# A macaron layer with two mixture-of-experts FFNs on one core: half the bias added on VectorE, TensorE's filling products redistributed, the logits of tiles 2 and 3 scored later, the first weight splits held behind the first gather

## The reference, cut to what matters

```
x = x + 0.5 * ffn(layernorm(x))        # first FFN,  f = 0
x = x + attention(layernorm(x))
x = x + 0.5 * ffn(layernorm(x))        # second FFN, f = 1

ffn(x):   logits = x @ router.T; the best 2 of 8 experts for each token, gates = softmax of the two
          out = sum over the 2 experts of gate * (silu(x @ wi_a.T) * (x @ wi_b.T)) @ wo.T
          return out + bias
attention: 16 heads of 16, causal, over 256 tokens, 4 batches; ctx @ w_o.T + b_o
```

## Time and profile before

| what | value |
|---|---|
| median of 3 runs | 430.71 us (430.55 to 431.05) |
| the profiled execution | 430.32 us |
| its span in the profile | 428.6 us |
| mean granted clock of TensorE | 0.975 |
| TensorE busy | 402.1 us, 94% |
| VectorE busy | 299.3 us, 70% |
| ScalarE busy | 257.1 us, 60% |
| GpSimd busy | 249.2 us, 58% |
| chain that ended last, by engine | TensorE 64%, VectorE 15%, DMA 8%, issue 5% |

### The profile page before, as it was taken

One profiled execution on the slowest core, in us unless ns is written; L12 is line 12 of the kernel. 1 busy time (PEld: TensorE's weight loads), 2 busy tenths in 40 slices (PEclk: granted clock), 3 DMA queues, 4 the chain that ended last, 5 costly groups with the idle time before them and its releaser, 6 DMA issues.

```text
span 428.6 us, 10138 instructions
## 1 busy us (share of the span) xinstructions
PE 402.1 (94%) x2892; PEld 331.2 (77%) x2893; DVE 299.3 (70%) x612; ACT 257.1 (60%) x640; POOL 249.2 (58%) x312
## 2 busy tenths in 40 slices
PE   7779999999999989799999999888899999999996
PEld 3558888888888767588888888674588888888884
DVE  6878997756655895877677676967356775566566
ACT  2737866565556455788788787722365555655552
POOL 5355457765478169577777677200555596654860
PEclk9889999999999999999999999966999999999999
DMA  7959911211111800000000000007641212112136
GB/s 253 400 143 397 363 55 40 66 44 61 55 46 38 271 32 2 1 3 3 2 0 0 0 0 0 2 1 254 208 153 50 61 40 66 57 49 55 43 99 219
DMA packets 22059, 38.90 MB, mean 91 GB/s; under 512 B 3217, under 2 KB 14737, under 8 KB 21777
## 3 DMA queue, kind: packets, MB, share of 16 engines
q1 hardware_dynamic: 17168, 24.41, 16.6%
q0 software_dynamic: 4576, 12.07, 9.4%
q10 hardware_dynamic: 288, 2.10, 1.3%
HBM read 29.37 MB, written 9.19 MB: 90 GB/s over the span
## 4 chain that ended last, share of the span: by engine, by line
PE 64%; DVE 15%; DMA 8%; issue 5%; ACT 3%; POOL 3%; ACTq 0%; SPq 0%; DVEq 0%; POOLq 0%
PE bank L1379 25%; PE bank L1401 12%; PE bank L1549 6%; PE bank L1389 4%; PE bank L1560 4%; DMA w_out<-y_scratch 3%; PE bank L1516 3%; PE bank L1355 2%; DMA unused_rows<-in_wr_t,own_row 2%; DMA arena<-xn_scratch,gather_row 1%; DVE arena L902 1%; DMA y_scratch<-arena,scatter_row 1%; DVE pT_lo L1185 1%; DVE v L1255 1%; PE bank L1550 1%
## 5 line engine op out<-in xcount | busy, mean ns | idle before, releaser
L533 POOL DMA_INDIRECT arena<-xn_scratch,gather_row x46 | 51.4, 1117 | 60.8 <-PE bank L1355 39.5
L539 POOL DMA_INDIRECT y_scratch<-arena,scatter_row x42 | 61.1, 1454 | 34.8 <-ACT arena L707 32.0
L1043 DVE TENSOR_TENSOR wo_lo<-w_out,wo_hi 128x1024 fp32r<-128x1024 f32 x46 | 61.2, 1330 | 4.1 <-PE bank L1401 2.5
L1379 PE MATMUL bank<-w_hi,xT_hi 128*128 x184 | 62.4, 421 | 0.0
L1048 DVE TENSOR_TENSOR gT_lo<-bank,gT_hi 128x512 fp32r<-128x512 f32 x46 | 31.7, 689 | 38.7 <-ACT gT_hi L681 38.7
L1379 PE MATMUL bank<-w_hi,xT_lo 128*128 x184 | 57.7, 394 | 0.0
L1379 PE MATMUL bank<-w_lo,xT_hi 128*128 x184 | 57.3, 392 | 0.0
L674 ACT ACTIVATE arena<-bank 128x512 f32<-128x512 f32 x46 | 27.5, 598 | 46.7 <-PE bank L1379 46.7
L619 POOL TENSOR_TENSOR k_head<-k_hi,head_mask 128x256 fp32r<-128x256 f32 x64 | 38.7, 625 | 28.1 <-PE bank L1550 21.0
L696 ACT ACTIVATE wo_hi<-w_out 128x1024 fp32r x46 | 48.8, 1061 | 5.5 <-issue 3.4
L1032 DVE TENSOR_TENSOR xT_lo<-bank,xT_hi 128x256 fp32r<-128x256 f32 x46 | 19.5, 424 | 35.8 <-ACT xT_hi L666 35.6
(11 more groups left out here) (197 smaller groups left out, 961.5 us busy)
## 6 DMA issues: line engine op xcount, KB each, us to landing
w_raw<-in_win_t SPq DMA_DIRECT2D x8, 1024.0 KB, 9.7
w_out<-in_wout_t SPq DMA_DIRECT2D x16, 512.0 KB, 7.8
w_out<-y_scratch SPq DMA_DIRECT2D x8, 512.0 KB, 6.2
xn_scratch<-arena ACTq DMA_DIRECT2D x2, 1024.0 KB, 6.0
x<-in_x SPq DMA_DIRECT2D x4, 256.0 KB, 3.7
out<-x SPq DMA_DIRECT2D x4, 256.0 KB, 2.1
arena<-xn_scratch,gather_row POOLq DMA_INDIRECT x46, 3.5
y_scratch<-arena,scatter_row POOLq DMA_INDIRECT x46, 3.0
```

The source lines that it names most:

```text
L533: pool.indirect_dma_start(out=xb[j % 2][:, :], out_offset=None, in_=xn_dram, in_offset=bass.IndirectOffsetOnAxis(ap=gather_row[:, j:j + 1] ...
L539: pool.indirect_dma_start(out=y_dram, in_=y[j % 2][:, :], in_offset=None, out_offset=bass.IndirectOffsetOnAxis(ap=scatter_row[:, j:j + 1], ...
L1043: dve.tensor_tensor(wo_lo[:, :, :], w_out[:, bass.ds(e, 1), :, :].rearrange("p o c d -> p (o c) d"), wo_hi[u][:, :, :].bitcast(F32), ALU.s ...
L1379: last = pe.matmul(bank[2 * half + u][:, :], tok[u][:, k, :], wts[:, bass.ds(e, 1), k, half * H:(half + 1) * H], start=(part == 0 and k == ...
```

## The change

It has five parts.

1. `bias_half` and GpSimd's `add_bias` of it go. VectorE adds half the bias itself, a pair of tiles at a time (`add_half_bias`): one pair after block 5's work, three pairs after block 6's.
2. The rehearsal goes, and with it GpSimd's wait for it.
3. VectorE holds its first splits (`split_low(0)`, `split_low(1)`) until GpSimd has raised `first_begun`, just behind its first gather.
4. The logits of tiles 2 and 3 in the second FFN are scored after the output projection and the transposes of tiles 4 and 5; `best_of` and `choose` of the first group move behind with them, `choose` behind the last `scale`.
5. The filling products change: one more after tiles 2 and 3 and one after tiles 4 and 5 of the first layer norm, 4 after the first FFN's last logits, 10 instead of 6 and 8 instead of 6 behind `plan_ready`; in the finish 3 between the two context transposes, 2 after the logits of tiles 4 and 5 in place of 2 before them, 1 before the last logits, and 4 instead of 2 after them.

```diff
-WARM_START, WARM_RANKS, WARM_PLAN, WARM_TURNED = 12, ((6, 5), (6, 5)), (6, 6), (4, 4)
-WARM_END, WARM_TURN2, WARM_CHOSEN = 2, 2, 2
+WARM_START, WARM_RANKS, WARM_PLAN, WARM_TURNED = 12, ((6, 5), (6, 5)), (10, 8), (4, 4)
+WARM_END = 2
 WARM_TURN = (5, 3)
-WARM_LN = (5, 1, 0, 0)
+WARM_LN = (5, 2, 1, 0)
+WARM_LAST = (4, 4)
+WARM_FINISH = (3, 2, 1)
...
-        bias_half = sb("bias_half", [P, D])
+        bias_row = sb("bias_row", [P, D])
...
@@ GpSimd
-            def rehearse():
-
-                then(pool.iota(own_row[:, :], [[0, 1]], base=0, channel_multiplier=1))
-                pool.indirect_dma_start(out=unused_rows[:, :], out_offset=None, in_=wr_in,
-                                        in_offset=bass.IndirectOffsetOnAxis(ap=own_row[:, 0:1], axis=0)).then_inc(rehearsed, 16)
...
-            rehearse()
...
             def ffn(f):
-                if f == 0:
-                    pool.wait_ge(rehearsed, 16)
                 pool.wait_ge(plan_ready, f + 1)
...
                 for j in range(AHEAD):
                     gather(f, j)
+                    if f == 0 and j == 0:
+                        pool.sem_inc(first_begun)
...
-                    if j == 6:
-                        if f == 0:
-                            pool.wait_ge(bias_loaded, 32)
-                            then(pool.tensor_scalar(bias_half[:, :], bias_half[:, :], 0.5, None, ALU.mult))
-                        add_bias(2 * f, bias_half)
-                    elif j == SCATTERED // 2:
+                    if j == SCATTERED // 2:
...
@@ VectorE
+            def add_half_bias(f, i):
+
+                dve.wait_ge(bias_loaded, 32)
+                dve.wait_ge(xn_ready, TILES * 2 * f + 2 * i + 2)
+                two = x[:, 2 * i:2 * i + 2, :]
+                dve.scalar_tensor_tensor(two, bc(bias_row[:, :], 1, [P, 2, D]), 0.5, two, ALU.mult, ALU.add)\
+                    .then_inc(bias_added, 1)
+
...
                 if f == 0:
+                    dve.wait_ge(first_begun, 1)
                     split_low(0)
                     split_low(1)
...
                     if isinstance(j, int) and j == PEELED - 2:
                         weigh_slots(f)
+                        add_half_bias(f, 0)
+                    if isinstance(j, int) and j == PEELED - 1:
+                        for i in range(1, TPAIRS):
+                            add_half_bias(f, i)
...
                 scale(2, 2)
-                best_at = best_of(1, 0)
...
                 sum_up(TPAIRS - 1, 1)
+                best_at = best_of(1, 0)
+                scale(2, TPAIRS - 1)
                 choose(0, best_at)
-                scale(2, TPAIRS - 1)
...
@@ TensorE, ffn(f): the part with f == 0, then the part with f == 1
                     score_experts(0, (TPAIRS - 1,))
+                    warm(WARM_LAST[0])
...
                         last.then_inc(xnT_in_psum, 1)
+                    warm(WARM_FINISH[2])
...
                     last.then_inc(logits_done, 1)
-                    warm(WARM_CHOSEN)
+                    warm(WARM_LAST[1])
...
@@ TensorE, finish()
                 turn_half(0)
-                score_experts(1, (1,))
+                warm(WARM_FINISH[0])
                 turn_half(1)
                 project_half(0)
                 project_half(1)
                 turn(2, (2,))
-                warm(WARM_TURN2)
+                score_experts(1, (1,))
 
                 pe.wait_ge(attn_added, BATCH + 1)
                 score_experts(1, (2,))
+                warm(WARM_FINISH[1])
```

More of the change, by code:

```diff
@@ L197, in build @@
         row_nos = sb("row_nos", [P, P], F16)
-        own_row = sb("own_row", [P, 1], I32)
-        unused_rows = sb("unused_rows", [P, E])
         blk_nos = sb("blk_nos", [P, BLOCKS + 1], F16)
@@ L283, in build @@
         half_hot = sem("half_hot")
-        rehearsed = sem("rehearsed")
+        first_begun = sem("first_begun")
         pairs_done = sem("pairs_done")
@@ L428, in _ @@
             load_w_out(E - 1)
-            for dst, src in ((bias_half, bias_in), (bo, bo_in)):
+            for dst, src in ((bias_row, bias_in), (bo, bo_in)):
                 sp.dma_start(dst[:, :], src.partition_broadcast(P)).then_inc(bias_loaded, 16)
```

## The result

The changed kernel takes **427.68 us** (median of 17 runs, 425.42 to 431.14) beside 430.62 of before (17 runs, 428.21 to 433.92): ratio 0.9947, 95% interval 0.9926 to 0.9969. Two further sets gave 427.45 and 427.47 us. It is faster, by 0.53% or 2.3 us by the ratio; the two medians differ by 2.9 us. 5.5 us were forecast.

What follows compares the result with a forecast made beforehand. TensorE's chain was taken to bound the whole program. The terms -1.1 (stall), -1.1 (start), +0.2, -2.9 (finish) and -0.6 (last logits) sum to -5.5 from 430.3: 424.8, median 425.2 us, range 424.0 to 428.9.

Steps and rivals of the forecast that it cites:

- sign: Whole kernel: faster, chance 0.9; same 0.05, slower 0.05.
- the start: First gather to block 0: rehearsal gone and splits held, gather lands 1.0 us sooner; -1.1 us, ends 0.2 and 1.6.
- handed over: Hold at the first gather: first_begun rises as the gather is handed over (21.5), xT_lo on time; gain 1.6 us.
- instruction ends: Hold at the first gather: first_begun rises when its instruction ends (22.4), hi*lo products wait 0.5; gain 1.1 us.
- Rival C: First gather: pays what the rehearsal paid, landing 7.52 us after its start instead of 3.31; median 429.8, chance 0.05.
- 0.5 earlier start: First gather: without the rehearsal GpSimd starts it at about 21.46 instead of 21.95 us.
- the last logits: Last logits of the finish: 1.73 to 0.96 us at full clock, less 0.15; -0.6 us, ends +0.5 and -0.8.
- The bias: Block 8, first FFN: GpSimd's bias add gone, so the stall goes, -1.1 us; bias on VectorE +0.2.
- the +0.2: Block 7, first FFN: three bias adds on VectorE make gT_lo end at 71.5, where TensorE wanted it at 71.29.
- The finish: First context transpose to the projection's closing addition: 6.16 us falls to about 3.2 at full clock; -2.9, ends -0.3 and -3.0.
- Rival A: Finish: clock stays low as now, finish gives -0.3 and tail -0.4; 427.6, median 428.0 us; chance 0.25.
- the logits' move alone: Finish: moving the logits of tiles 2 and 3 gives about 0.75 to 1.2 us of the -2.95, the rest the clock.

Runs made afterwards that it cites:

- the hold behind the instruction: Changed kernel with first_begun raised by a GpSimd memset behind the first gather: 428.86 us (0.9977); with xT_lo also behind expert 0's splits alone, 427.78 us (0.9976).
- finish alone: Before with only part 4 and the fillers of the finish and behind it, 8 instead of 6 behind the second plan_ready: 428.25 us (0.9968).
- moved logits without fillers: Changed kernel without the finish's new fillers, 2 instead of 4 behind the last logits, logits of tiles 2 and 3 still moved: 429.70 us (0.9964).
- bias alone: Before with only part 1, half the bias on VectorE and GpSimd's halving and add gone, run twice: 429.50 us (1.0001) and 427.96 us (0.9970).

## Why the prediction was right in sign and wrong in size

**The failed step: the start** (-1.1 predicted, about +0.7 measured). "So it ends near 22.4 instead of 23.44" took for granted that the hold keeps the splits off the gather's instruction. Both cases that I weighed there ("handed over" and "instruction ends") had it 0.94 long. In truth `first_begun` rose at the hand-over, so the splits started 0.2 us ahead of the instruction and it ended 2.3 us behind their start. Where the splits started later it ended later: they started 0.22 us behind `gather_row`'s end without the hold, 0.60 and 0.67 with it, and the instruction ended 0.40 and 0.46 later with it. The rehearsal's absence adds 0.3. With no split beside it (the hold behind the instruction) the gather's instruction took 1.24 us. Rival C was right in kind and far off in size: 1.24 us is also the rehearsal's own time, against 0.94 for later ones. In place of the 0.5 earlier start that I booked for the missing wait, the gather starts 0.88 us behind `gather_row`'s end, where it was 0.77. The wait had held nothing up: it is 0.77 or 0.78 in all nine traces with a rehearsal, whether that landed at 20.4 or at 21.5. I also took the clock to be full at block 0, and it wasn't. That alone is worth more than the edit: finish alone, whose start is that of before, has no fall there and needs 7.35 us from `gather_row` to block 0's second half, where before has 8.54; the changed kernel has 9.22 with a fall, and 7.69 with 18 fillers and none. (One profile without a fall, moved logits without fillers, has 8.83; its `xT_hi` came 1.1 us later than in that one.) Whether fillers prevent that fall isn't shown: it stands between 25 and 28 us in 5 of 6 profiles with 6 of them behind `plan_ready`, in 6 of 10 with 10, and in none of 3 with 16 or 18.

**The second failed step: the last logits** (-0.6). The 0.73 us was gained (1.00 against 1.73), and given back 9 us later, as the gather then met more of the store and reload, and landed at the same distance from the store. I priced each stage to its own end and not to the transfer that the next one waits for.

**The bias** (-1.1 and +0.2) was right in place: the third piece is 78.0 us in all 16 traces that have it and 79.1 to 79.3 in the three that don't; the +0.2 did not show. `gT_lo` of block 7 ended at 71.69, and its product, the third part of a `combine` that began at 71.04, started at 72.07 with no wait.

**The finish** (-2.9) came out in the two first profiles: 12.39 to 8.84 us to `chosen` is -3.55 with the last logits' -0.6 in it. Rival A, a fall in the finish as before, occurred in part in 4 of the 15 profiles of kernels that have part 4 (there the piece took 10.15 to 10.33 us). Nor is before's 12.39 the rule: its own finish took 12.39, 12.39, 11.66 and 10.52 in the four profiles that have it (before and bias alone). The means are 11.74 and 9.23, so part 4 with the last logits is worth about 2.5 us and not 3.5. Nearly all of it is the clock:

| kernels | us at clock 0.50 in the piece | the piece, us |
|---|---|---|
| before, twice | 9.0 | 12.39 |
| bias alone, first and second | 8.1, 3.4 | 11.66, 10.52 |
| part 4, four profiles | 3.1 to 3.4 | 10.15 to 10.33 |
| part 4, eleven profiles | 0 to 1.5 | 8.84 to 9.02 |

With the same 3.4 us of low clock the old order takes 10.52 and the new one 10.33 at most, so the order and its fillers by themselves give 0.2 to 0.4 us (one trace of the old order against four). For the logits' move alone I had put 0.75 to 1.2, up to the projection's end, and +0.15 behind it. I had called the rest the clock, and so it is, but before's first profile, from which I took 6.16 and 1.73, had one of the two longest falls of the four. That the term fits it is partly luck, and so is the median near rival A's 428.0: A's fall did not happen in 11 of 15.

**The sum.** From the two first profiles the edited places give +0.7 - 1.1 - 3.55 + 0.9 = -3.1 us, with the mean of the finish -2.0; measured were -2.3 by the ratio. In the changed kernel's profile a low clock took 1.75 us in the attention and 1.65 at the second FFN's first block (4.30 against 2.65), more than that gain; ten of its 17 runs were 2.0 to 4.7 us shorter. The other traces bear out that it is the clock: with a fall near 180 us the attention piece takes 127.55 to 128.73 us (8 traces), without one 126.78 to 127.40 (11); with one at 302 to 303.4 us the last piece takes 4.26 to 4.31 (5), without one 2.60 to 2.68 (14). I had booked no term for falls outside the places that I edited. Which place a fall takes differs between executions, and what decides it these runs don't show.

**What the hold was for.** The gather's instruction took 1.24 us with no split beside it and 1.66 to 2.13 with them, the rehearsal missing in all. I had followed the rows there, rightly, and then gone wrong on when the hold opens. VectorE's `wo_lo` beside GpSimd's bias add took 4.36 to 4.38 us in the three traces that have that add there, and 1.23 in the changed kernel.

## What to carry to other kernels

A semaphore raised by GpSimd's queue behind an indirect DMA said here that it was handed over, not that it ran (the held work began 0.2 us ahead of it). Raised by an instruction of the same engine behind the DMA, it held the work off (the splits began at 23.37, 0.15 us behind the instruction's end at 23.22); then ask whether the held work has that time to give. Where a stage ends in a transfer behind other transfers, as the second FFN's first gather does, shortening the work between them can move its issue and leave its landing where it was (here 0.76 us nearer to the store's issue, and the transposes 12.50 us behind that against 12.40): measure the distance from the first transfer of the queue. When an edit's worth is a clock that stays up, compare the mean clock and time over many runs, and use a profile only piece by piece.

## What the runs showed of the hardware that I had not expected

- An indirect DMA's instruction on GpSimd that starts beside a row of VectorE subtractions of 1.16 us each ended a fixed time behind the start of the first: 2.04 to 2.06 us with a rehearsal before it (9 traces), 2.32 to 2.34 without (8 traces), whether it started 0.17 or 0.66 us behind it. Half of the four subtractions' 4.63 us is 2.31. Why it ends ahead of that after a rehearsal is open.
- The first indirect DMA of the program cost 0.1 us more before its start (0.88 against 0.77 behind `gather_row`) and 0.3 us more in its instruction (1.24 against 0.94, with no split beside either).
- With more filling products in the waits the mean granted clock over the runs was higher (0.982, 0.988 to 0.992, 0.994 with 6, 10 and 18 behind the first plan; the kernels differ in other fillers too).
- A low clock cost less on average than in a place where TensorE is the path. There it was 1.65 us for 3.4 us at 0.50 (the second FFN's block 0). Over 335 runs of all kernels here, each against the mean of its own set, a run with 1 us more at 0.50 (from its mean clock and span) took 0.29 us more, and runs of one kernel still differ by 1 us (standard deviation) at the same clock. By that slope the changed kernel's 10 us less at 0.50 (mean clock 0.990 over its 38 runs against 0.977) are worth some 3 us, an estimate, which is about the whole gain; by it the bias add's 1.1 and what the start lost nearly cancel.
